# Graph attention over a sparse 8192 x 8192 adjacency: whole row tiles of 32 KB rows in three slots, a loop body of six groups, and two moves in the tail

## The reference, cut to what matters

```
x: [8192, 128] f32;  adj: [8192, 8192] int32, ones with probability 0.000244, else 0
h = x @ W;  a1 = a[:128, 0];  a2 = a[128:, 0]
e = (h @ a1)[:, None] + (h @ a2)[None, :]
e = where(e > 0, e, 0.2 * e);  e = where(adj > 0, e, -9e15)
h_prime = softmax(e, axis=1) @ h
y = x + elu(h_prime)
out = (y - mean(y)) / sqrt(var(y) + 1e-5)      # per row of 128
```

## Time and profile before

| | |
|---|---|
| median of three runs | 719.43 us (718.99 to 722.22) |
| the profiled execution | 721.3 us, span from first to last instruction 719.5 us |
| PE, DVE, ACT, POOL busy | 557.4, 480.7, 520.5, 443.6 us |
| moved in all | 285.57 MB, mean 397 GB/s |
| transfers of adj | 127 of 2 MB, two of 1 MB, 15.9 us from issue to landing |
| mean granted TensorE clock | 0.88 of full speed |

### The profile page before, as it was taken

How to read it: one execution, slowest core, us unless ns; L and a number is a source line. 1 busy time by engine, 2 the same in 40 slices (tenths; PEclk the granted TensorE clock), 3 DMA queues, 4 the chain that set the end, 5 groups by cost and what they waited for, 6 DMA issues and landing times.

```text
span 719.5 us, 11920 instructions
## 1 busy us (share of the span) xinstructions
PE 557.4 (77%) x3071; PEld 351.2 (49%) x3071; DVE 480.7 (67%) x2051; ACT 520.5 (72%) x414; POOL 443.6 (62%) x668
## 2 busy tenths in 40 slices
PE   0858799987778887778888787887778787777884
PEld 0323455554455554555455554554455554544583
DVE  1474777767766667667667667677766667667565
ACT  0847578787878777887878787878878777878511
POOL 2016267766766676676667676667666766777741
PEclk9987798899999999998889999799999999999957
DMA  9999999999999999999999999999999999999901
GB/s 353 326 422 422 384 413 429 427 422 425 428 425 429 426 426 429 425 427 425 428 426 427 427 428 427 428 426 426 428 425 428 429 427 428 426 423 424 284 17 31
DMA packets 34582, 285.57 MB, mean 397 GB/s; under 512 B 5512, under 2 KB 13856, under 8 KB 18048
## 3 DMA queue, kind: packets, MB, share of 16 engines
q1 hardware_dynamic: 29008, 276.83, 92.1%
q0 software_dynamic: 5120, 8.42, 3.3%
q10 hardware_dynamic: 432, 0.07, 0.1%
HBM read 283.18 MB, written 4.19 MB: 399 GB/s over the span
## 4 chain that ended last, share of the span: by engine, by line
DMA 63%; PE 12%; ACT 10%; DVE 6%; issue 5%; POOL 2%; SPq 0%; ACTq 0%; POOLq 0%; DVEq 0%
DMA adj_sb<-in_adj 60%; ACT adj_squared L551 10%; PE fold L653 7%; DMA a_sb<-in_L_gnn_a 2%; PE misc L678 2%; PE fold L649 1%; POOL edge_row L362 1%; PE x_att_ps L701 1%; DMA nb<-in_x,index 1%; DVE s_all L838 1%; PE small L668 1%; DVE x_times_wa L836 1%; DVE top_map L852 0%; DVE spread L374 0%; POOL nb L497 0%
## 5 line engine op out<-in xcount | busy, mean ns | idle before, releaser
L551 ACT ACTIVATE adj_squared<-adj_sb 128x4096 bf16<-128x4096 int32 x128 | 462.4, 3613 | 103.2 <-DMA adj_sb<-in_adj 97.2
L653 PE MATMUL fold<-adj_sb,bit_ident 128*128 128x512 bf16 x1024 | 302.0, 445 | 0.0
L497 POOL DMA_INDIRECT nb<-in_x,index x160 | 165.7, 1036 | 92.4 <-issue 64.2
L653 PEld LDWEIGHTS fold<-adj_sb,bit_ident 128*128 128x128 bf16 x1024 | 109.4, 107 | 150.6 <-issue 61.0
L649 PE MATMUL fold<-col_no,ident_bf 128*128 128x512 bf16 x128 | 53.2, 416 | 114.2 <-DMA adj_sb<-in_adj 101.7
L852 DVE MAX8 top_map<-fold 128x8 f32<-128x512 f32 x128 | 89.5, 699 | 67.1 <-PE fold L653 62.4
L362 POOL TENSOR_SCALAR edge_row<-row_iota,edge_in 128x128 f32<-128x128 int32 x186 | 129.4, 710 | 0.0
L378 POOL TENSOR_TENSOR spread<-edge_row,edge_w 128x384 f32<-128x384 f32 x60 | 51.9, 885 | 66.4 <-DVE edge_w L965 66.3
L477 POOL TENSOR_SCALAR empty_diag<-ident,counts 128x128 f32<-128x128 f32 x64 | 42.2, 665 | 68.5 <-DVE counts L889 35.4
L649 PEld LDWEIGHTS fold<-col_no,ident_bf 128*128 128x128 bf16 x128 | 16.4, 128 | 129.1 <-issue 101.4
L701 PEld LDWEIGHTS x_att_ps<-spread,nb 128*128 128x128 f32 x372 | 58.6, 225 | 9.8 <-issue 4.7
(11 more groups left out here) (120 smaller groups left out, 623.4 us busy)
## 6 DMA issues: line engine op xcount, KB each, us to landing
adj_sb<-in_adj SPq DMA_DIRECT2D x127, 2048.0 KB, 15.9
out<-x_sb SPq DMA_DIRECT2D x2, 1536.0 KB
nb<-in_x,index POOLq DMA_INDIRECT x160
adj_sb<-in_adj SPq DMA_DIRECT2D x2, 1024.0 KB, 15.1
out<-x_sb SPq DMA_DIRECT2D x5, 128.0 KB
out<-x_sb SPq DMA_DIRECT2D x1, 384.0 KB
W_sb<-in_L_gnn_W ACTq DMA_DIRECT2D x1, 64.0 KB, 7.9
x_sb<-in_x SPq DMA_DIRECT2D x4, 0.5 KB, 17.7
```

The lines of the kernel that those rows point to most:

```text
L497: nc.gpsimd.indirect_dma_start(out=nb_of(j, g)[:, c, :], out_offset=None, in_=x[:, :], in_offset=bass.IndirectOffsetOnAxis(ap=index[:, g, ...
L551: nc.scalar.activation(adj_squared[:, h % 2, :], adj_sb[:, h % LOAD_SLOTS, :], ACT.Square, accum_out=half_sum[:, h:h + 1]).then_inc(square ...
L653: last = nc.tensor.matmul(fold[:, h % LOAD_SLOTS, :], bit_ident[:, b, :], adj_low[:, h % LOAD_SLOTS, b * FOLD:(b + 1) * FOLD, 0], start=Fa ...
```

## The change

- A slot now holds a whole row tile: three slots (TILE_SLOTS = 3) of 32 KB per partition, 12 MB for 8 MB, and one 4 MB transfer per tile whose rows are contiguous 32 KB. A slot is refilled once both its halves have been squared and folded, and both halves wait for the one landing. Only the last tile comes in three pieces (its first half, and two quarters of the tile).
- To make room, `adj_squared` is one buffer in place of two, and `x_times_wa` is half as large: `own_scores` runs in eighths of x, four in each of the first two steps; `mean_row` comes one step earlier.
- The loop body has six groups (GROUPS = 6). Six steps are written out, four passes of the body follow, then the two last steps and the tail. What `g` indexed in buffers is now `g % SETS` with SETS = 2, so those buffers are the same, and the PSUM banks are still four (BANKS).
- In the tail DVE does `indices(final)` before `neighbour_scores(back1)`.
- SP waits for the last gathers before its first store.

The core of the diff (the other hunks put `g % SETS` for `g`, `prior(j, g, n)` for the tests on the first groups, and N_GROUPS for BODIES * GROUPS):

```diff
-    GROUPS = 2
+    SETS = 2
+    GROUPS = 6
     BODY = PAIR * GROUPS
-    BODIES = TILES // BODY
+    N_GROUPS = TILES // PAIR
+    BODIES = (N_GROUPS - 2) // GROUPS
     HALVES = 2 * BODY
-    LOAD_SLOTS = 4
+    BANKS = 4
+    TILE_SLOTS = 3
+    LOAD_SLOTS = 2 * TILE_SLOTS
...
-        adj_squared = sb("adj_squared", [P, 2, HALF], bf16)
-        x_times_wa = sb("x_times_wa", [P, TILES // 4, D], fp32)
+        adj_squared = sb("adj_squared", [P, HALF], bf16)
+        x_times_wa = sb("x_times_wa", [P, TILES // 8, D], fp32)
...
         def steps(eng, step):
-            for n in range(3 * GROUPS):
-                step(n // GROUPS, n % GROUPS)
-            with eng.Fori(3, BODIES - 1) as i:
+            for g in range(GROUPS):
+                step(0, g)
+            with eng.Fori(1, BODIES) as i:
                 for g in range(GROUPS):
                     step(i, g)
...
-                    for h in range(g * 2 * PAIR, (g + 1) * 2 * PAIR):
-                        if not (first(i) and h < LOAD_SLOTS):
-                            sp.wait_ge(squared, i * HALVES + (h + 1 - LOAD_SLOTS))
-                            sp.wait_ge(folded, i * HALVES + (h + 1 - LOAD_SLOTS))
-                        parts = 2 if is_final(i, g) and h == HALVES - 1 else 1
-                        size = HALF // parts
-                        for k in range(parts):
-                            lo = (h % 2) * HALF + k * size
-                            tile = adj_tiles[bass.ds(i * BODY + h // 2, 1), :, lo:lo + size]
-                            nc.sync.dma_start(adj_sb[:, h % LOAD_SLOTS, k * size:(k + 1) * size],
-                                              tile.rearrange("o p c -> (o p) c")).then_inc(
-                                                  rest_loaded if k else loaded[h % LOAD_SLOTS], 16)
+                    for t in range(g * PAIR, (g + 1) * PAIR):
+                        if not (first(i) and t < TILE_SLOTS):
+                            sp.wait_ge(squared, i * HALVES + 2 * (t + 1 - TILE_SLOTS))
+                            sp.wait_ge(folded, i * HALVES + 2 * (t + 1 - TILE_SLOTS))
+                        slot = t % TILE_SLOTS
+                        space = adj_sb[:, 2 * slot:2 * slot + 2, :].rearrange("p s c -> p (s c)")
+                        tile = adj_tiles[bass.ds(i * BODY + t, 1), :, :].rearrange("o p c -> (o p) c")
+                        if is_last_half(i, 2 * t + 1):
+                            rest = HALF + HALF // 2
+                            nc.sync.dma_start(space[:, 0:HALF], tile[:, 0:HALF]).then_inc(loaded[slot], 16)
+                            nc.sync.dma_start(space[:, HALF:rest], tile[:, HALF:rest]).then_inc(rest_loaded[0], 16)
+                            nc.sync.dma_start(space[:, rest:N], tile[:, rest:N]).then_inc(rest_loaded[1], 16)
+                        else:
+                            nc.sync.dma_start(space, tile).then_inc(loaded[slot], 16)
...
+                sp.wait_ge(gathered[final[1] % SETS], uses(*final) + 16 * CHUNKS)
                 for lo, hi in STORES:
...
                 def square_half(i, g, q):
                     h = g * 2 * PAIR + q
-                    act.wait_ge(loaded[h % LOAD_SLOTS], landings(i, h))
                     if is_last_half(i, h):
-                        act.wait_ge(rest_loaded, 16)
-                    if not (first(i) and h < 2):
-                        act.wait_ge(squared, i * HALVES + (h - 1))
+                        for part in rest_loaded:
+                            act.wait_ge(part, 16)
+                    else:
+                        act.wait_ge(loaded[h // 2 % TILE_SLOTS], landings(i, h))
+                    if not (first(i) and h < 1):
+                        act.wait_ge(squared, i * HALVES + h)
...
                 def fold_half(i, g, q):
                     h = g * 2 * PAIR + q
-                    pe.wait_ge(loaded[h % LOAD_SLOTS], landings(i, h))
-                    if not (first(i) and h < LOAD_SLOTS):
-                        pe.wait_ge(picked, i * HALVES + (h + 1 - LOAD_SLOTS))
+                    if is_last_half(i, h):
+                        pe.wait_ge(rest_loaded[0], 16)
+                    else:
+                        pe.wait_ge(loaded[h // 2 % TILE_SLOTS], landings(i, h))
+                    if not (first(i) and h < BANKS):
+                        pe.wait_ge(picked, i * HALVES + (h + 1 - BANKS))
...
-                    if first(i):
-                        own_scores(2 * g)
-                        own_scores(2 * g + 1)
-                    if isinstance(i, int) and (i, g) == (1, 0):
+                    if first(i) and g < 2:
+                        for q in range(4 * g, 4 * g + 4):
+                            own_scores(q)
+                    if first(i) and g == 2:
                         mean_row()
...
                 route(*final)
+                indices(*final)
                 neighbour_scores(*back1)
-                indices(*final)
                 scores(*back1)
                 weights(*back1)
```

More of the change, by code:

```diff
@@ L254, in graph_attention @@
         weights_loaded = sem("weights_loaded")
-        loaded = [sem(f"loaded{s}") for s in range(LOAD_SLOTS)]
-        rest_loaded = sem("rest_loaded")
-        gathered = [sem(f"gathered{g}") for g in range(GROUPS)]
+        loaded = [sem(f"loaded{s}") for s in range(TILE_SLOTS)]
+        rest_loaded = [sem(f"rest_loaded{k}") for k in range(2)]
+        gathered = [sem(f"gathered{g}") for g in range(SETS)]
         out_stored = sem("out_stored")
@@ L368, in spread_weights @@
             hold(eng, edge_w_ready, count(j, g), spare)
-            if not (first(j) and g == 0):
+            if prior(j, g, 1):
                 hold(eng, summed, count(j, g) - 1, spare)
@@ L473, in mark_empty @@
                     hold(pool, listed, count(j, g), pool_spare)
-                    if not first(j):
-                        hold(pool, summed, count(j, g) - GROUPS, pool_spare)
+                    if prior(j, g, SETS):
+                        hold(pool, summed, count(j, g) - SETS, pool_spare)
                     for t in range(PAIR):
-                        last = nc.gpsimd.tensor_scalar(empty_diag[:, g, t, :], ident[:], found[:, t:t + 1], None,
+                        last = nc.gpsimd.tensor_scalar(empty_diag[:, g % SETS, t, :], ident[:], found[:, t:t + 1], None,
                                                        ALU.is_gt)
@@ L492, in gather @@
                     hold(pool, indexed, count(j, g), pool_spare)
-                    if not first(j) and not is_final(j, g):
-                        hold(pool, summed, count(j, g) - GROUPS, pool_spare)
+                    if prior(j, g, SETS) and not is_final(j, g):
+                        hold(pool, summed, count(j, g) - SETS, pool_spare)
                     for c in range(CHUNKS):
@@ L559, in exp_elu @@
                     act.wait_ge(h_made, count(j, g))
-                    if not first(j):
-                        act.wait_ge(h_read, count(j, g) - GROUPS)
-                    nc.scalar.activation(z_exp[:, g, :, :], h_of(j, g)[:, :, 0:D], ACT.Exp).then_inc(elu_exp, 1)
+                    if prior(j, g, SETS):
+                        act.wait_ge(h_read, count(j, g) - SETS)
+                    nc.scalar.activation(z_exp[:, g % SETS, :, :], h_of(j, g)[:, :, 0:D], ACT.Exp).then_inc(elu_exp, 1)
                 def copy_sums(j, g):
                     act.wait_ge(summed, count(j, g))
-                    if not (first(j) and g == 0):
+                    if prior(j, g, 1):
                         act.wait_ge(h_made, count(j, g) - 1)
@@ L709, in times_W @@
                     pe.wait_ge(x_att_ready, count(j, g))
-                    if not (first(j) and g == 0) and not is_late(j, g):
+                    if prior(j, g, 1) and not is_late(j, g):
                         pe.wait_ge(h_read, count(j, g) - 1)
@@ L961, in edge_weights @@
                     dve.wait_ge(share_sent, count(j, g))
-                    if not (first(j) and g == 0):
+                    if prior(j, g, 1):
                         dve.wait_ge(spread_ready, count(j, g) - 1)
-                    v.after(nc.vector.tensor_tensor(own_share[:], share_ps, at_slot[:, g, :, :], ALU.mult))
+                    v.after(nc.vector.tensor_tensor(own_share[:], share_ps, at_slot[:, g % SETS, :, :], ALU.mult))
                     nc.vector.reduce_sum(edge_w[:], own_share[:], AX.X).then_inc(edge_w_ready, 1)
@@ L974, in finish @@
                     dve.wait_ge(h_read, count(j, g))
-                    if not first(j):
-                        dve.wait_ge(norm_ready, count(j, g) - GROUPS)
+                    if prior(j, g, SETS):
+                        dve.wait_ge(norm_ready, count(j, g) - SETS)
                     v.after(nc.vector.scalar_tensor_tensor(x_sb[:, mine, :], elu[:], -1.0, x_sb[:, mine, :],
```

141 lines of the change are left out of this document (72 added, 69 removed).

## The result

The changed kernel takes 756.98 us (median of 4 runs, 755.60 to 757.49) against 720.46 us for the kernel before on the same chip: a ratio of 1.0503, 95% interval 1.0472 to 1.0534, so 36 us slower. The forecast was 733.2 us with a range of 714 to 746 (the forecast's own range was 721 to 748): the direction was right, the size was not. The profiled execution took 755.6 us, its span 753.7.

A forecast was written before the change was run, and what follows sets the result against it. The adj stream bounds the kernel at 20.26 us per group; the slower gather loop would take over. Last landing +0.1 (-4.9 - 2.2 + 7.2), end backlog +13.7: 719.43 + 13.8 = 733.2 us, own range 721 to 748, 8-in-10 range 714 to 746.

The forecast's parts named there:

- a tile as the unit: End of stream: the last tile's first half can no longer be folded while the second travels; +3.1 us taken.
- Body of six groups: Main loop: fewer taken branches, DVE's idle time there already hidden by the stream; 0 us.
- the rival: Code fetches in the six-group body stall DVE or PE at three branches; +13 us at most, chance 0.07.
- The gather loop: Gathers, scores, indices: longer bursts under 32 KB rows raise it from 16.1 to 21.9 us, above the stream's 20.1.
- +13.8: Whole kernel: total forecast slowdown, 0.1 us at the last landing plus 13.7 us of compute behind it.
- -4.9: Adj stream: longer rows mean fewer row packets and signals, gaining 4.9 us; lower end 0.
- 0.3 us per group: Main loop: estimated loss after dry moments let gather packets pass, over about 24 groups; +7.2 us, bounds 0 to +22.
- paid back at the end: After the last landing: the buffer's slack returns as compute backlog, last fold 16.0 us behind instead of 2.3; +13.7 us.
- The hole of 80 to 92 us: Stream stall from `own_scores` early on: a third more buffer covers it; -2.2 us, between 0 and -2.2.
- The tail: Last groups: `indices(final)` first gains 0, at most 2.4 us; stores behind the last gathers, 0.
- One `adj_squared`: Main loop on ACT: each square waits for its predecessor's signal, but they run in order anyway; 0 us.
- the weights at the start: Start: small weight packets take turns with 32 KB rows, PE and ACT start some 3 us later; 0, at most +3.

The follow-up runs named there:

- body6_nb0: Kernel before with the six-group loop body and `nb` put back on a multiple of 512 bytes by unused bytes: 741.21 us, 1.0287.
- one_row_more: Kernel before, with SP also loading one 16 KB row into an unused tile in each of 30 groups: 736.20 us, 1.0214.
- unrolled_nb0: Changed kernel with all steps written out (no loop) and `nb` back on a multiple of 512 bytes: 739.76 us, 1.0252.
- six_halves_unrolled_nb0: Changed kernel without loop, `nb` on a multiple of 512 bytes, six half-tile slots of 16 KB rows, each freed by itself: 731.50 us, 1.0156.
- rows16: Changed kernel with each row tile loaded by two transfers of 16 KB rows, the slot staying a whole tile: 753.69 us, 1.0450.
- sixteen_rows_more: Kernel before, with SP also loading sixteen rows (256 KB) into an unused tile in each of 30 groups: 839.66 us, 1.1616.
- after_nb0: Changed kernel with `nb` back on a multiple of 512 bytes, all else as it is: 751.60 us, 1.0407.
- ahead: Changed kernel with `indices(p1)` moved ahead of `neighbour_scores(p2)` in every step: 807.29 us, 1.1207.

## Why the prediction was wrong

The kernels make a walk from one to the other, in ratios to the kernel before (1% is 7.2 us; a step of 0.4% or less is not told from nothing, and another order of the steps could share them out otherwise):

| step | from | to | us |
|---|---|---|---|
| straight code in place of the two-group loop | 1 | 1.0170 | +12 |
| 12 MB, start and tail (half-tile slots) | 1.0170 | 1.0156 | -1 |
| a tile as the unit | 1.0156 | 1.0205 | +3.5 |
| 32 KB rows | 1.0205 | 1.0252 | +3.5 |
| a loop of six groups, three taken branches | 1.0252 | 1.0407 | +11 |
| `nb` 64 bytes further | 1.0407 | 1.0503 | +7 |

**The step that failed** is "Body of six groups": "Fewer taken branches ... hidden by the stream; 0". It is 23 of the 36 us by this table, 30 with the address that it moved; the direct way, before to body6_nb0, measures 1.0287, 21 us, and leaves 9 us (to 1.0407) for buffer, tile, rows and tail. I had seen that 200 to 640 us held no instruction queue and that no row showed whether three times the code fits, and then took the end of that open question that cost nothing; the rival gave it 0.07 and at most 13 us. Two mechanisms replace it. The first is shown: at each of the three taken branches DVE stands for 6.0 to 6.9 us (19.5 us in four waits), more than the 4.2 us that I found spare, and the stream runs dry: slices of 306 and 303 GB/s. Written out, the waits go and 11 us with them.

The second is in part argued: code that streams by costs through the DMA engines even where no compute engine is seen to wait. Against the kernel before, the written-out one has 17 more q8 packets and 22 more q14 packets on its page (26 and 35 for 9 and 13), 448 KB; at 0.61 us per 16 KB this is 17 us, if all fall to one engine. An estimate from q8's own packets is higher: 16 of them take 0.2% of 16 x 440 us in 200 to 640 us, some 0.9 us each, which makes it 22. Measured were 12, as one_row_more measured 15 for 18. The changed kernel has 3 and 22 more, some 9 us by the first count; but its tail shows no late engine (share 0.01 in its window of 694 to 706 us), so what these packets cost it by this way stays open. That q14 packets share the late engine is supported by one packet in 670 to 682 us of the half-tile version; for q8 it is inferred from the size of the loss.

The Trainium skill ("Runtime: NRT & Kernel Launch", Instruction fetch mechanics) says that a branch out of the buffered pages stalls, and the trace agrees (6.9 us before `z_one`, 0.3 in all once written out). It also says that a long kernel's code streams in with its cost mostly hidden, and prefers full unrolling. Here the measurement decides: written out, this kernel loses 1.7%. That its landings hang on the engine that carries the code is the likely reason, seen in one tail only.

**The gather loop** was right in every sign and too dear in its sum. Rows moved as one packet; 0.61 became 1.2 us a turn; the burst of the group shown is 12.2 us for 6.9 (forecast 5.5 to 6.1 more) and is read 4.9 us later; DVE waits for them 18 times; the last fold ends 15 us after the last landing (forecast 16). The forecast for all this was +13.8 (the -4.9 and -2.2 included); tile and rows together measure +7. The 0.3 us per group was near: 419 GB/s in the loop of unrolled_nb0 make 8.65 MB take 20.64 us, 0.38 more than before, code packets included, and the bursts of 5.2 us beside 11.6 show the relief at work. The +13.7 "paid back at the end" is the term that was too dear: in unrolled_nb0 the last square starts at 688.08 us, 9 us after its transfers are over (2 GB/s from 679 on); without tiles and long rows, in six_halves_unrolled_nb0, it starts at 683.52, because there the landing itself is late. The backlog moves it by 4.6 us. Two delays that run side by side do not add.

**What I left out of the loop**: PE idles while it waits for the scores, and its granted clock then falls. unrolled_nb0 has 0.84 in the loop, six_halves_unrolled_nb0 0.89. The same twelve products of `send_scores` take 2.70 us in the first, at a granted clock of 0.50 (1.2 GHz) after a wait of 1.88, and 1.49 in the second, at 1.00 (2.4 GHz) behind other products without a wait. What this costs the kernel no run separates:

```profile
498.56 2.70 PE L694 MATMUL misc<-t_slot,edge_row 128*128 128x10 f32 x12 [1.88 <-DVE t_slot L950]
```

```profile
492.05 1.49 PE L687 MATMUL misc<-t_slot,edge_row 128*128 128x10 f32 x12
```

**The smaller steps.** The address of `nb` was no step at all: I had taken the longer `half_sum` for free. `mean_row` did not move: it stands in the third step of both kernels. The hole of 80 to 92 us closed as forecast (431 GB/s); what that is worth is 0.16%, not 2.2 us. The tail: 0 forecast, 0.9995 measured. One `adj_squared` was not tried by itself. Nor were the weights at the start: the changed kernel's PE waits for them some 5 us longer (25.9 for 20.5, and 20.5 again in rows16), so it comes with the 32 KB rows; what it costs at the end is not shown.

## What to carry to other kernels

- A loop whose trace shows no instruction queue is worth something in itself: a change that lengthens its body must be priced, in stalls at the branch (here 6 to 7 us) and in code packets beside the stream (0.3 us per 8 KB). Here unrolling cured the first and about doubled the second.
- A mean DMA share of 1.0 does not say that the stream is at its best: it hides one late engine (look for a tail at 1/16 share at the end of the stream) and it hides longer packets (0.99 at 369 GB/s in sixteen_rows_more). The share, times 16 engines and the length of the window, over the number of row packets gives the time of one, and tells the two apart.
- Before two kernels are compared, compare the addresses of what small DMAs write; 64 bytes of an unrelated tile moved this one by 1.3%.

## What the hardware showed that I had not expected

- A gather target 64 bytes past a multiple of 512 lengthens the mean 16 KB row packet of a full stream from 0.616 to 0.625 us, and the kernel by 9.9 us.
- One packet of 16 KB more per group costs 0.5 us of the whole program (30 for 15 us); a 256 KB transfer over 16 partitions costs 3.9 us and lengthens the mean row of the stream from 0.616 to 0.70 us. The cause is open.
- The stall at a branch hardly depends on the length of the rows in the queue: at most 6.9, 5.7 and 5.8 us with 32 KB rows (the changed kernel, after_nb0, ahead), 6.3 and 5.9 with 16 KB.
